# Third attention of a four-layer kernel: next keys in the scores' banks, one next query head in a bank of turned weights, two low parts of value products ahead of an addition

## The reference

```python
q = (query @ Wq).reshape(nb, q_len, H, D).transpose(0, 2, 1, 3)     # query = layernorm(x)
k = (key @ Wk).reshape(nb, q_len, KVH, D).transpose(0, 2, 1, 3)     # key = value = ctx
v = (value @ Wv).reshape(nb, q_len, KVH, D).transpose(0, 2, 1, 3)
q = q * cos + _rotate_half(q) * sin
k = k * cos + _rotate_half(k) * sin
k = jnp.repeat(k, GROUPS, axis=1)
v = jnp.repeat(v, GROUPS, axis=1)
scores = jnp.einsum('bhqd,bhkd->bhqk', q, k) / jnp.sqrt(jnp.float32(D))
scores = jnp.where(mask == 0, jnp.float32(-1000000000.0), scores)
attn = jax.nn.softmax(scores, axis=-1)
x = jnp.einsum('bhqk,bhkd->bhqd', attn, v)
return x.transpose(0, 2, 1, 3).reshape(nb, q_len, H * D) @ Wo
```

## Time and profile before

| | |
|---|---|
| median of 3 runs | 1810.57 us (1807.59 to 1816.55) |
| profiled execution | 1806.27 us, its span 1805.0 us |
| TensorE busy | 1638.7 us, 91% of the span |
| mean granted TensorE clock | 0.955 of full speed |
| DVE, POOL, ACT busy | 57%, 32%, 28% |
| first and last transpose or matmul with the split weights of the third attention | 630.2 to 1280.1 us of the span |

### The profile page before, as it was taken

How to read it: one execution, slowest core, us unless ns; L and a number is a source line. 1 busy time by engine, 2 the same in 40 slices (tenths; PEclk the granted TensorE clock), 3 DMA queues, 4 the chain that set the end, 5 groups by cost and what they waited for, 6 DMA issues and landing times.

```text
span 1805.0 us, 21297 instructions
## 1 busy us (share of the span) xinstructions
PE 1638.7 (91%) x8900; PEld 1182.1 (65%) x8900; DVE 1024.2 (57%) x1328; ACT 501.1 (28%) x744; POOL 579.4 (32%) x370
## 2 busy tenths in 40 slices
PE   8899989998799889989999998999799877779998
PEld 2264358886388677767777777778655445548886
DVE  6987852224715645555455645545551488476666
ACT  4130020103422124323232333322112377630000
POOL 4817732220544223223131313311040144562221
PEclk9989999999999979989999999999989999889999
DMA  2000041002000310101011010100301011400000
GB/s 119 1 1 1 1 164 47 24 1 123 12 1 1 117 35 24 36 24 59 0 59 35 25 36 24 36 1 1 142 0 24 0 36 38 179 1 7 13 13 18
DMA packets 18016, 66.49 MB, mean 37 GB/s; under 512 B 1440, under 2 KB 9760, under 8 KB 13312
## 3 DMA queue, kind: packets, MB, share of 16 engines
q1 hardware_dynamic: 17920, 65.12, 10.4%
HBM read 58.82 MB, written 2.10 MB: 34 GB/s over the span
## 4 chain that ended last, share of the span: by engine, by line
PE 69%; DVE 15%; POOL 7%; ACT 5%; issue 3%; DMA 1%; SPq 0%; DVEq 0%; ACTq 0%; POOLq 0%
PE banks L270 42%; PE banks L264 21%; POOL arena L1545 3%; PE banks L399 2%; DVE arena L1387 2%; DVE arena L442 1%; PE banks L1835 1%; POOL grouped_split L1564 1%; DVE arena L234 1%; POOL w_lo L2298 1%; ACT arena L1479 1%; ACT arena L1478 1%; PE banks L2097 1%; ACT dense L1943 1%; POOL arena L1550 1%
## 5 line engine op out<-in xcount | busy, mean ns | idle before, releaser
L270 PE MATMUL banks<-grouped_split 128*128 128x512 f32 x1536 | 394.2, 411 | 16.0 <-DVE grouped_split L1415 9.9
L270 PEld LDWEIGHTS banks<-grouped_split 128*128 128x128 f32 x1536 | 293.8, 196 | 84.0 <-DVE grouped_split L1415 9.4
L1545 POOL TENSOR_TENSOR arena<-arena,grouped 128x512 f32<-128x512 f32 x80 | 105.3, 1321 | 386.4 <-ACT arena L1479 386.3
L270 PE MATMUL banks<-experts_split 128*128 128x512 f32 (+1 forms) x792 | 180.0, 389 | 1.9 <-DVE experts_split L627 1.9
L270 PEld LDWEIGHTS banks<-experts_split 128*128 128x128 f32 (+1 forms) x792 | 146.1, 185 | 35.1 <-DVE experts_split L624 2.1
L1383 DVE TENSOR_TENSOR arena<-banks,grouped 128x512 f32<-128x512 f32 x80 | 54.6, 682 | 171.9 <-ACT arena L1479 171.9
L264 PE MATMUL banks<-arena 128*128 128x64 f32 (+2 forms) x730 | 129.6, 332 | 8.3 <-DMA arena<-in_c 6.4
L264 PEld LDWEIGHTS banks<-arena 128*128 128x128 f32 x730 | 116.7, 215 | 31.0 <-issue 18.6
L1387 DVE TENSOR_TENSOR arena<-arena 128x512 f32<-128x512 f32 x80 | 89.4, 1118 | 63.8 <-POOL arena L1545 62.8
L655 DVE SCALAR_TENSOR_TENSOR arena<-banks,experts,arena 128x512 f32<-128x512 f32 x64 | 47.8, 750 | 111.3 <-PE banks L270 111.2
L264 PE MATMUL banks<-dense 128*32 128x64 f32 (+4 forms) x1738 | 88.7, 307 | 23.2 <-ACT dense L1943 9.2
(11 more groups left out here) (288 smaller groups left out, 3005.6 us busy)
## 6 DMA issues: line engine op xcount, KB each, us to landing
grouped<-in_attn SPq DMA_DIRECT2D x16, 1024.0 KB, 5.0
experts<-in_expert SPq DMA_DIRECT2D x8, 1024.0 KB, 4.9
linear<-in_ffn SPq DMA_DIRECT2D x1, 4096.0 KB, 15.0
grouped<-in_attn SPq DMA_DIRECT2D x8, 512.0 KB, 3.6
dense<-arena SPq DMA_DIRECT2D x16, 256.0 KB, 4.9
dense<-in_w SPq DMA_DIRECT2D x1, 3584.0 KB, 12.1
dense<-in_attn SPq DMA_DIRECT2D x1, 3072.0 KB, 12.7
dense<-in_w SPq DMA_DIRECT2D x1, 2688.0 KB, 10.2
```

Of the source, the lines that this page charges most:

```text
L270: s = pe.matmul(dst, lhsT=lhsT[i], rhs=rhs[j], start=(k == 0 and x == 0), stop=(k == n - 1 and x == 2))
L1545: g_.tensor_tensor(rot, rot, f(SIN + h * HALF, HALF), ALU.mult).then_inc(rot_sin.sem, 1)
```

## The change

- Keys of the next group no longer stand in the ring of four banks, but in bank 4 (first half) or 5 (second half), between one reading and the next writing of the scores. Query head 0 of the next group stands in bank 6. The other uses go round banks 0 to 3 as before (`ring`, `place`). The first group's keys and its head 0 stay in the ring.
- TensorE gets the waits that belong to it: for the reading of the scores, for the copy of the turned weights, and for the cosine products before those banks are written again.
- POOL makes the low part of the next query weights in two pieces of 1024 columns (steps 0 and 1, steps 2 and 3), and TensorE waits for each piece at its step.
- The scores of the second half are made as 16 after the third step and 16 after the fourth step of the next head 0. TensorE's wait for the addition of head 3 moves from before the head to behind its third step.
- On DVE the rotation is split in `rotary_cos` and `rotary_add`. The order becomes: cosine product of head 3, cosine product of the next keys, low parts 0 and 1, addition of head 3, low parts 2 and 3, addition of the next keys.
- The last group has no next keys or heads. Its scores wait for the same addition, and its DVE order is the new one.

```diff
+    ring = [u for u in uses if u[1] == 0 or u[0] != "k" and (u[0], *u[2:]) != ("q", 0, 0)]
+    at_ring = {u: n for n, u in enumerate(ring)}
...
+    def place(u):
+        return at_ring[u] % NB if u in at_ring else 6 if u[0] == "q" else 4 + u[2]
...
             if g + 2 < G2:
-                sp.wait_ge(*wq_lo(g + 1))
+                sp.wait_ge(*wq_lo(2 * g + 2))
                 group_load(sp, g + 2, 0, 2048, STG_Q, q_in)
...
         def take(u):
-            n = at_use[u]
-            if n >= NB:
-                old = uses[n - NB]
+            if u not in at_ring and u[0] == "k":
+                pe.wait_ge(*score_read(2 * u[1] - 1 + u[2]))
+            elif u not in at_ring:
+                pe.wait_ge(*turn_out(4 * u[1] - 3))
+            elif at_ring[u] >= NB:
+                old = ring[at_ring[u] - NB]
                 if old[0] == "v":
                     pe.wait_ge(*bank_a(2 * old[1] + old[2] + 1))
                 else:
                     vector_has(pe, old)
-            return bank[:, n % NB, :]
+            return bank[:, place(u), :]
...
-        def q_rows(g, q, h, between=None):
+        def q_rows(g, q, h, between=None, pieces=False):
             to = take(("q", g, q, h))
             for c in range(DC):
+                if pieces and c % 2 == 0:
+                    pe.wait_ge(*wq_lo(2 * g - 1 + c // 2))
...
+                if h == 1 and k == 0 and g + 1 < G2:
+                    vector_has(pe, ("q", g + 1, 0, 0))
...
             apply(g, 0)
-            pe.wait_ge(*rot_add(at_turn["q", g, 3, 1] + 1))
             pe.wait_ge(*score_read(2 * g + 1))
+
+            def second_scores(c):
+
+                if c == 2:
+                    vector_has(pe, ("k", g + 1, 0, 0))
+                    pe.wait_ge(*rot_add(at_turn["q", g, 3, 1] + 1))
+                if c >= 2:
+                    score(1, 2 * c - 4)
+                    score(1, 2 * c - 3)
+
             if nxt:
-                pe.wait_ge(*wq_lo(g + 1))
-                q_rows(g + 1, 0, 0, lambda c: score(1, c))
+                q_rows(g + 1, 0, 0, second_scores, pieces=True)
             else:
+                pe.wait_ge(*rot_add(at_turn["q", g, 3, 1] + 1))
                 for c in range(DC):
                     score(1, c)
...
             rotary(("q", g, 2, 1))
-            rotary(("q", g, 3, 1))
+            rotary_cos(("q", g, 3, 1))
             if nxt:
-                rotary(("k", g + 1, 0, 0))
-            apply_low(g, 0)
+                rotary_cos(("k", g + 1, 0, 0))
+            apply_low(g, 0, range(2))
+            rotary_add(("q", g, 3, 1))
+            apply_low(g, 0, range(2, 4))
+            if nxt:
+                rotary_add(("k", g + 1, 0, 0))
...
                 g_.wait_ge(*wq_hi(g + 2))
-                g_.tensor_tensor(wqs[1], f(STG_Q, LQ), wqs[0].bitcast(F32), ALU.subtract).then_inc(wq_lo.sem, 1)
+                for lo in (0, LQ // 2):
+                    cut = slice(lo, lo + LQ // 2)
+                    g_.tensor_tensor(wqs[1][:, cut], f(STG_Q, LQ)[:, cut], wqs[0][:, cut].bitcast(F32),
+                                     ALU.subtract).then_inc(wq_lo.sem, 1)
```

More of the change, by code:

```diff
@@ L1372, in vector, with rotary_cos, rotary_add @@
         v.wait_ge(*rope_out(4))
-        def rotary(u):
-            n, i, h = at_use[u], at_turn[u], u[2] if u[0] == "k" else u[3]
+        def rotary_cos(u):
+            i, h = at_turn[u], u[2] if u[0] == "k" else u[3]
+            v.wait_ge(*rot_copied(i + 1))
+            v.tensor_tensor(f(QC + i % 2 * HALF, HALF), bank[:, place(u), :], f(COS + h * HALF, HALF),
+                            ALU.mult).then_inc(bank_v.sem, 1)
+        def rotary_add(u):
+            i, h = at_turn[u], u[2] if u[0] == "k" else u[3]
             rot, qc = f(ROT + i % 2 * HALF, HALF), f(QC + i % 2 * HALF, HALF)
@@ L1381, in rotary @@
                 rot, qc = (x.rearrange("p (b s) -> p b s", b=8) for x in (rot, qc))
-            v.wait_ge(*rot_copied(i + 1))
-            v.tensor_tensor(f(QC + i % 2 * HALF, HALF), bank[:, n % NB, :], f(COS + h * HALF, HALF),
-                            ALU.mult).then_inc(bank_v.sem, 1)
             v.wait_ge(*rot_sin(i + 1))
@@ L1387, in rotary @@
             v.tensor_tensor(to, qc, rot, ALU.add).then_inc(rot_add.sem, 1)
+        def rotary(u):
+            rotary_cos(u)
+            rotary_add(u)
         def softmax_top(g, h):
@@ L1406, in softmax_sum, with apply_low @@
             v.reciprocal(tot, tot).then_inc(sum_done.sem, 1)
-        def apply_low(g, h):
-            for j in range(4):
+        def apply_low(g, h, pieces=range(4)):
+            for j in pieces:
                 u = ("a", g, h, j)
@@ L1414, in apply_low @@
                 v.wait_ge(*at_hi(8 * g + 4 * h + j + 1))
-                v.tensor_tensor(lo, bank[:, at_use[u] % NB, :].rearrange("p (b h q) -> p b h q", b=2, h=QH2),
+                v.tensor_tensor(lo, bank[:, place(u), :].rearrange("p (b h q) -> p b h q", b=2, h=QH2),
                                 hi.bitcast(F32), ALU.subtract).then_inc(bank_v.sem, 1)
@@ L1421, in output_add @@
             v.wait_ge(*use_mm(at_use[u] + 1))
-            v.tensor_tensor(x, bank[:, at_use[u] % NB, :], x, ALU.add).then_inc(bank_v.sem, 1)
+            v.tensor_tensor(x, bank[:, place(u), :], x, ALU.add).then_inc(bank_v.sem, 1)
         for u in uses[0:6]:
@@ L1472, in rotary @@
         def rotary(u):
-            n, i = at_use[u], at_turn[u]
+            i, b = at_turn[u], place(u)
             rot = f(ROT + i % 2 * HALF, HALF)
-            act.wait_ge(*use_mm(n + 1))
+            act.wait_ge(*use_mm(at_use[u] + 1))
             if i >= 2:
                 act.wait_ge(*rot_add(i - 1))
-            act.activation(rot[0:64, :], bank[64:P, n % NB, :], ACT.Copy)
-            act.activation(rot[64:P, :], bank[0:64, n % NB, :], ACT.Copy).then_inc(rot_copied.sem, 1)
+            act.activation(rot[0:64, :], bank[64:P, b, :], ACT.Copy)
+            act.activation(rot[64:P, :], bank[0:64, b, :], ACT.Copy).then_inc(rot_copied.sem, 1)
         def exps(g, h):
@@ L1486, in v_rows @@
         def v_rows(g, h):
-            n = at_use["v", g, h, 0]
-            act.wait_ge(*use_mm(n + 1))
-            act.activation(f(VN + h * HALF, HALF), bank[:, n % NB, :], ACT.Copy).then_inc(bank_a.sem, 1)
+            u = "v", g, h, 0
+            act.wait_ge(*use_mm(at_use[u] + 1))
+            act.activation(f(VN + h * HALF, HALF), bank[:, place(u), :], ACT.Copy).then_inc(bank_a.sem, 1)
         def turn(g, h):
@@ L1497, in apply_high @@
             for j in range(4):
-                n = at_use["a", g, h, j]
+                u = "a", g, h, j
                 k, b2 = j // 2, j % 2
                 hi = ats[0][:, :, 2 * k * P:(2 * k + 2) * P].rearrange("p h (b c q) -> p b h c q", b=2, c=2)[:, :, :, b2, :]
-                act.wait_ge(*use_mm(n + 1))
-                act.activation(hi, bank[:, n % NB, :].rearrange("p (b h q) -> p b h q", b=2, h=QH2),
+                act.wait_ge(*use_mm(at_use[u] + 1))
+                act.activation(hi, bank[:, place(u), :].rearrange("p (b h q) -> p b h q", b=2, h=QH2),
                                ACT.Copy).then_inc(at_hi.sem, 1)
```

## The result

The changed kernel took 1784.66 us in the median (four runs, 1782.34 to 1793.23), beside 1813.56 for the kernel before: a ratio of 0.9869 with a 95% interval of 0.9841 to 0.9896. Measured once more beside other kernels it took 1778.79 (six runs) against 1810.02, a ratio of 0.9829, 0.9799 to 0.9859. By the two ratios it is faster by 24 and by 31 us, where 38 had been forecast; both intervals stay clear of 1. Both medians lie in the range, above the 1770.

What follows compares the result with a forecast made beforehand. TensorE was taken to bound the kernel (69% of the chain). Pauses 22.8 plus half clock 20.0, less 3.0 (new pause) and 1.85 (last group), save 38 us: 1806.3 to 1768.3, called 1770; range 1763 to 1776, with rivals 1762 to 1790.

Steps and rivals of the forecast that it cites:

- The pauses of 3.02 and 0.71 us: TensorE before the second pair of value products and before next query head 0: both go; stretches' pauses total 22.8 us.
- The half clock as their consequence: TensorE at clock 0.76 to 0.90 in groups 1 to 6: returns to 1.00 without the pauses, saving 20.0 us.
- The seven stretches: Groups 0 to 6, first weight transposes to first output product: 134.01 us long, 22.82 of pauses and 19.98 of half clock.
- POOL's two pieces: Low part of next query weights: two pieces of 2.5 us, ready 1.5 and 0.6 us before TensorE wants them, cost 0.
- The new wait for head 3's addition: TensorE after the head's third step: 0.5 us pause in each of groups 1 to 6, 3.0 us in all.
- The last group: No keys follow, nothing gained; its scores wait for head 3's addition behind two low parts: loss 1.85 us.
- The second half: Second half of a group: 1.04 us pause stays, with the 0.7 before it and the low clock that followed once.
- the side branch of the first: Within rival 1 (pauses go, clock falls anyway; 0.13): one clock fall in the last group alone, up to 4.7 us.
- late low parts: Rival 2: POOL also locks out DVE's low parts, pause 1.8 instead of 0.5, 7.8 us more, 1778; chance 0.10.
- no new pause: Rival 3: DVE gets in ahead of POOL or TensorE comes later, 3.0 us more gained, 1767; 0.67 together with forecast.
- another wait in the place of the old: Rival 4: second value pair waits equally long for another bank owner; only the 0.71 pauses go, 1804; chance 0.06.
- more clock loss than before: Slower case: clock falls at the third step's wait and in the second half of every group, 1836; chance 0.04.

Runs made afterwards that it cites:

- the banks alone: Changed kernel with only the new places of keys and head 0; POOL's single subtraction, VectorE's order and score places as before: 1782.21 us, ratio 0.9850.
- the addition first: Changed kernel, but VectorE adds head 3 right after its cosine product in every group, ahead of the keys' cosine product and low parts: 1773.14 us, ratio 0.9759.

## Why the prediction came out as it did

*The pauses of 3.02 and 0.71 us* went as worked out: the second pair waits for nothing, the head neither.

*The half clock as their consequence* was right, and is shown by the kernel before with its long pause filled. The seven stretches saved 39.1 us, where the sum had 22.8 + 20.0 − 3.0 = 39.8. What carried the sum was one row of windows.

*POOL's two pieces* were in time for TensorE, as said. They were not 2.5 us each but 2.80 and 2.38, 5.14 together.

*The new wait for head 3's addition* came from the mechanism named, the addition behind the keys' sine product. It was 0.71 to 0.74 us, not 0.5; about 0.1 of that is POOL's pieces, 5.14 us for the 5.0 of the sum, which put off the sine product and with it the addition. Part of the difference came back: group 0 needed 12.72 us where 13.03 was taken. With the banks alone, where the scores still come eight by eight, it needed 12.83 beside its pause of 1.47, so the scores in sixteens account for 0.1 at most.

*The last group* is the term that was mis-sized: "Loss 1.85 us". The wait was right (1.80 when nothing hides it), but the group lost 7.1 and, in the second profile, 5.8 us. Not all of this is the late addition's: in the mean of the profiles with and without it, the loss is 4.4. The rest is a fall behind the 2.60 us wait, which came ahead of the new wait in both profiles, and which the one profile of the kernel before happened not to have. The text saw the danger and left it out of the sum, as a fall "once in the last group alone" worth up to 4.7. In all five profiles with the late wait there was half clock in the last group. The two waits, 2.6 and 1.8 us, 2 us apart, look like the kernel before's 3.02 and 0.71, which went with a fall in six groups of six; that comparison was in the text, and it should have decided the sum.

*The second half* kept its pauses, as said, and a fall that had been counted once came twice in one profile and five times in the other, 1.6 us each. That is chance as far as can be seen: over ten kernels' profiles with these pauses it followed 23 of 70 of them, over four without them none of 28.

*The rest.* The spans saved 24.0 and 27.7 us in the two profiles. From 38, the stretches take 0.7. The last group takes 5.3 in the first profile and 4.0 in the second, the second halves 1.6 and 6.2. The stages that the change doesn't touch add 6.2 us in the first profile and save 0.6 in the second. Which falls an execution gets, and why those stages scatter, stays open. Of the rivals, only the side branch of the first came true, in the last group; late low parts, no new pause, another wait in the place of the old, and more clock loss than before did not.

## What to carry to other kernels

A pause of the engine that bounds the kernel may cost twice: as itself, and as the slow clock behind it. Look at the granted clock in the stretch after each pause, and fill the pause with idle work to see what it is worth without its causes. Look also at where in the stretch the clock falls: a fall ahead of a wait was not brought by it.

Where an order is changed for the groups of a loop, work out the last one by itself: here it had none of the gain and got a new wait, and it lost 6 to 7 us in the two profiles, about 4 of them by the new order, while the other groups won 39. When a bank is short, look for banks that stand idle between two uses by another stage: that move alone gave the whole gain here as far as the medians tell, and two more uses moved in the same way took another 18 us out of the attention.

## What the runs showed of the hardware

- A VectorE instruction with two SBUF operands that waits for POOL goes in between two POOL instructions that follow one another at once. In the kernel with the addition first, POOL's second piece took 2.85 us in place of 2.38 when an addition did so; the first piece took 2.80 in both kernels, behind the addition of head 2. Splitting POOL's instruction of 4.96 us in two cost 0.18 us in all (5.14) and opened that gap.
- The fall of TensorE's clock after a pause is not decided by the pause's length alone. The same 2.60 us wait, with full speed before it, stands unfilled in the last group of twelve profiles. In seven of them a fall began between 0.7 us before its end and 1.3 us behind it; in five none did before the next wait. Without the late addition, where nothing follows soon, the half clock lasted 3.4 us in three profiles and 13.7 us in one, and four had none. Two waits of 1.04 and 0.7 us near each other were followed by a fall about one time in three. One wait of 1.47 us (banks alone) or of 0.73 us (changed kernel) in each of groups 1 to 6 was followed by none.
